# Smaller weight chunks, a fifth staging buffer and two moved waits in the heads of a two-block attention kernel

## The reference, cut to what matters

```python
for _ in range(NB):                                   # NB = 2
    logits = _rms(x, norm_pre_w) @ compete_w.T + compete_b
    vals, idx = top_k(swapaxes(logits, 1, 2), 4)
    wgt = softmax(vals)
    wx = x @ write_w.T + write_b
    ws = _rms(ws + einsum('bsk,bskd->bsd', wgt, gathered(wx, idx)), norm_post_w)
    q = x @ wq.T + bq;  kk = ws @ wk.T + bk;  vv = ws @ wv.T + bv
    att = softmax(einsum('blhd,bshd->bhls', q, kk) * scale)
    x = _rms(x + (att @ vv) @ out_proj_w.T + out_proj_b, norm_post_w)
out = x_in + x
```

## Time and profile before

| | us |
|---|---|
| median of 3 runs | 1086.61 (1082.34 to 1092.57) |
| the profiled execution | 1089.83 |
| its span, first to last instruction | 1087.8 |
| mean granted TensorE clock, share of full | 0.983 |
| first head, block start to first softmax add of its tail | 382.3 to 466.6 |
| second head, the same | 763.9 to 850.9 |
| write projection starts, first and second head | 398.9, 777.9 |
| tile 0's scores on PE (L1032, 16 records), each tail | 3.69 |
| K projection starts, first and second head | 408.2, 787.3 |

### The profile page before, as it was taken

The page is one execution under the profiler, slowest core; times in us unless marked ns, Lnnn a source line. Parts: engine busy times, 40 slices in busy tenths (PEclk is TensorE's granted clock), DMA queues, the critical chain, the costliest instruction groups (busy, mean ns, idle before and its releaser), DMA issues. The chain is left out here.

```text
span 1087.8 us, 14736 instructions
## 1 busy us (share of the span) xinstructions
PE 1017.6 (94%) x4984; PEld 574.4 (53%) x4984; DVE 724.1 (67%) x1004; ACT 574.7 (53%) x960; POOL 458.6 (42%) x214
## 2 busy tenths in 40 slices
PE   2999999999999888999999999997988999999995
PEld 0444444444444334466666666664344666666663
DVE  5999999999999532245555555553423366666664
ACT  3788988888888601235555555555111223333323
POOL 7899999999999310001111111111100033333333
PEclk9999999999999999999999999998898999999998
DMA  4456565656564769835566575646586566868664
GB/s 144 150 178 209 172 215 168 220 163 219 165 217 149 270 233 374 286 130 181 178 231 207 191 246 181 232 155 246 201 338 244 189 216 238 286 229 294 220 228 154
DMA packets 124412, 232.54 MB, mean 214 GB/s; under 512 B 8096, under 2 KB 82976, under 8 KB 122048
## 3 DMA queue, kind: packets, MB, share of 16 engines
q1 hardware_dynamic: 122560, 221.27, 59.1%
q10 hardware_dynamic: 1152, 8.39, 2.2%
q0 software_dynamic: 640, 2.10, 0.7%
HBM read 139.45 MB, written 92.28 MB: 213 GB/s over the span
## 5 line engine op out<-in xcount | busy, mean ns | idle before, releaser
L1032 PE MATMUL bank<-work 128*128 128x256 f32 (+1 forms) x1024 | 244.4, 382 | 3.4 <-DMA work<-x0T_scratch 1.8
L1061 PE MATMUL bank<-work 128*128 128x512 f32 (+1 forms) x512 | 230.3, 592 | 2.1 <-ACT work L1163 1.3
L1032 PEld LDWEIGHTS bank<-work 128*128 128x128 f32 x1024 | 187.2, 190 | 40.5 <-issue 20.6
L1223 POOL TENSOR_TENSOR work<-work 128x1024 f32<-128x1024 f32 x32 | 75.5, 2360 | 236.5 <-DVE work L1145 236.5
L1213 POOL COPY xres<-work 128x1024 f32<-128x1024 f32 x32 | 33.4, 1043 | 328.1 <-DVE work L1145 328.1
L455 PE MATMUL bank<-work,ident 128*128 128x512 f32 x256 | 126.9, 619 | 23.8 <-DVE work L370 22.5
L1061 PEld LDWEIGHTS bank<-work 128*128 128x128 f32 x512 | 97.1, 190 | 97.6 <-issue 91.8
L1096 DVE TENSOR_TENSOR work<-bank,sbias 128x256 f32<-128x256 f32 x64 | 27.2, 424 | 168.4 <-PE bank L1032 168.4
L440 POOL TENSOR_TENSOR work<-work 128x1024 f32<-128x1024 f32 x32 | 85.2, 2662 | 23.7 <-ACT work L355 8.2
L455 PE MATMUL bank<-work 128*128 128x511 f32 x192 | 91.4, 599 | 0.0
L434 POOL TENSOR_SCALAR work<-work 128x1024 f32<-128x1024 f32 x32 | 89.1, 2784 | 3.8 <-DMA work<-in_kT 1.2
(11 more groups left out here) (158 smaller groups left out, 1566.8 us busy)
## 6 DMA issues: line engine op xcount, KB each, us to landing
work<-in_kT SPq DMA_DIRECT2D x32, 512.0 KB, 3.4
work<-in_xT SPq DMA_DIRECT2D x32, 512.0 KB, 3.9
x0T_scratch<-work SPq DMA_DIRECT2D x32, 512.0 KB, 3.2
x_natural_scratch<-xres SPq DMA_DIRECT2D x32, 512.0 KB, 5.1
work<-x0T_scratch SPq DMA_DIRECT2D x32, 512.0 KB, 4.4
x_natural_scratch<-work SPq DMA_DIRECT2D x32, 512.0 KB, 3.1
x1T_scratch<-work SPq DMA_DIRECT2D x32, 512.0 KB, 2.8
work<-x1T_scratch SPq DMA_DIRECT2D x32, 512.0 KB, 4.9
```

Of the source, the lines that this page charges most:

```text
L1032: last = nc.tensor.matmul(ps_s[p], xTb[p][:, c, :], Amat[:, i, :, c * 32:c * 32 + 32], start=(c == 0), stop=(c == NC - 1))
L1061: last = nc.tensor.matmul(ps_o[:, cols], attT[:, k * P:(k + 1) * P], Bmat[k][:, i, cols], start=(k == 0), stop=(k == 1), skip_group_check= ...
L1223: nc.gpsimd.tensor_tensor(x1s[p], x1s[p], xo[p], ALU.add).then_inc(fin, 1)
```

## The change

1. `stream`: the five 2 MB loads become 20 of 512 KB, each with a semaphore per slot and chunk. Chunk a waits until PE has used chunk a of the half before it in that slot (`project` now counts per chunk) and until chunk a of the previous half in the stream has landed, so at most four are under way. PE waits per chunk. The `wo_T` loads become eight of 512 KB.
2. `stageA` gets a fifth buffer (at work[16384]); the copy of pair i waits for the store of pair i - 5.
3. PE waits for the copies of all products before group 2, not before group 0.
4. The stage of group (1, 2) moves to `lgT`, which is also the bias of the first four copies, so that this copy waits for them (`grp_d` 4). Tile 1's buffer is thereby free in the head.
5. SP loads tiles 0 and 1 in the head; PE computes tile 0's scores there in place of three `keep_warm` matmuls; the tail begins without them. SP's `wait_Bm` moves to tile 2.
6. The waits for the stores of x0T and x1T leave the ends of the first stage and of `tail(0)`; they stand now in the head, before SP's `load_x`, and in the second head before POOL's gathers also.

```diff
-        w_in = [stage_sem(head_sems, f"head_weights_in_{i}") for i in range(3)]
-        first_in = [stage_sem(head_sems, f"head_first_weights_in_{i}") for i in range(3)]
+        w_in = [[stage_sem(head_sems, f"head_weights_in_{i}_{a}") for a in range(4)] for i in range(3)]
...
-                sp.wait_ge(x0_out, 16 * NT)
...
-        stageA = [cut(14336 + 512 * i, 512) for i in range(4)]
-        stageB = {(0, 2): cut(8192, 1024), (0, 3): cut(8192, 1024), (1, 2): cut(2048, 1024), (1, 3): cut(8192, 1024)}
+        stageA = [cut(14336 + 512 * i, 512) for i in range(5)]
+        NA = len(stageA)
+        stageB = {(0, 2): cut(8192, 1024), (0, 3): cut(8192, 1024), (1, 2): lgT[:], (1, 3): cut(8192, 1024)}
...
+            stream = ((0, wk_T, 1, wr_ps, 0, 2), (1, wv_T, 0, wr_ps, 1, 2), (2, wv_T, 1, kk_ps, 0, 2),
+                      (0, wq, 0, kk_ps, 1, 3), (1, wq, 1, vv_ps, 0, 3))
...
-                    for slot, w, i, free, count in ((0, wk_T, 1, wr_ps, 1),
-                                                    (1, wv_T, 0, wr_ps, 2), (2, wv_T, 1, kk_ps, 1),
-                                                    (0, wq, 0, kk_ps, 2), (1, wq, 1, vv_ps, 1)):
-                        sp.wait_ge(free, count)
-                        piece(slot, w, i)
+                    for n, (slot, w, i, free, used, load) in enumerate(stream):
+                        for a in range(4):
+                            sp.wait_ge(free, 4 * used + a + 1)
+                            if n > 0:
+                                sp.wait_ge(w_in[stream[n - 1][0]][a], 16 * stream[n - 1][5])
+                            sp.dma_start(ring[slot][:, a, :], w[:, 4 * i + a, :]).then_inc(w_in[slot][a], 16)
...
                             sp.wait_ge(grp_ps, 4)
-                            load_x(sp, t, 0, 0, 0, 0)
+                            sp.wait_ge(x0_out if t == 0 else x1T_out, 16 * NT)
+                            for m in range(2):
+                                load_x(sp, t, 0, m, m, m)
...
                         for c in range(4 * i, 4 * i + 4):
+                            pe.wait_ge(w_in[slot][c % 4], 16 * load)
...
-                        last.then_inc(done, 1)
+                            last.then_inc(done, 1)
...
-                        if hp % 4 == 0:
-                            pe.wait_ge(w_in[hp // 4], 16 * 2)
+                        pe.wait_ge(w_in[hp // 4][hp % 4], 16 * 3)
...
-                    wait_product(pe, HP - 1)
...
+                        if g == 2:
+                            wait_product(pe, HP - 1)
...
                     wait_product(pe, HP - 2)
-                    keep_warm(banks[0], 3)
+                    wait_product(pe, HP - 1)
+                    pe.wait_ge(bias_in[t], 16)
+                    pe.wait_ge(xT_in[t][0], 16)
+                    for c in range(NC):
+                        last = nc.tensor.matmul(banks[0][:, 0:HS], xTb[0][:, c, :], Amat[:, 0, :, c * 32:c * 32 + 32],
+                                                start=(c == 0), stop=(c == NC - 1))
+                    last.then_inc(sc_ps, 1)
...
-                    wait(eng, st_a[i % 4], 16 * (i // 4))
+                    wait(eng, st_a[i % NA], 16 * (i // NA))
...
-                                eng.wait_ge(st_a[j], 16 * 2)
+                                eng.wait_ge(st_a[j], 16 * ((HP - 1 - j) // NA + 1))
...
+                    if (k, b) == (1, 2):
+                        eng.wait_ge(grp_d, 4)
...
+                    if t == 1:
+                        pool.wait_ge(x1T_out, 16 * NT)
...
-                        act.wait_ge(prod_ps, i + 2)
-                        act.dma_start(ring[i // 4][:, i % 4:i % 4 + 2, :], wo_T[:, i:i + 2, :])\
-                            .then_inc(wo_in[i // 2], 16)
+                        for j in (i, i + 1):
+                            act.wait_ge(prod_ps, j + 1)
+                            act.dma_start(ring[j // 4][:, j % 4, :], wo_T[:, j, :]).then_inc(wo_in[j], 16)
...
-                        if not (isinstance(m, int) and m == 0):
+                        if not (isinstance(m, int) and m < 2):
                             wait(sp, sc_ps, m - 1)
                             load_x(sp, t, b, tc, m, p)
+                        if isinstance(m, int) and m == 2:
+                            wait_Bm(sp)
...
-                    wait_Bm(sp)
...
-                        sp.wait_ge(x1T_out, 16 * NT)
...
-                    scores(0, 0, 0)
-                    scores(0, 0, 1)
```

More of the change, by code:

```diff
@@ L552, in head @@
             c_in, np_in, st_s = hsem("constants_in"), hsem("npost_in"), hsem("bias_out")
-            wo_in = [hsem(f"wo_in_{i}") for i in range(4)]
-            st_a = [hsem(f"A_out_{i}") for i in range(4)]
+            wo_in = [hsem(f"wo_in_{i}") for i in range(HP)]
+            st_a = [hsem(f"A_out_{i}") for i in range(NA)]
+            sc_ps = stage_sem(tail_sems, "tail_scores_ps")
             lgt_ps, lgT_ok, dtop, sel_ok, idx_ok = (hsem(x) for x in ("lgt_ps", "lgT", "top", "sel", "index"))
@@ L637, in _ @@
                             sp.wait_ge(grp_ps, 4)
-                            load_x(sp, t, 0, 0, 0, 0)
-                    for i in range(4):
-                        sp.wait_ge(st_a[i], 16 * 2)
+                            sp.wait_ge(x0_out if t == 0 else x1T_out, 16 * NT)
+                            for m in range(2):
+                                load_x(sp, t, 0, m, m, m)
+                    for i in range(NA):
+                        sp.wait_ge(st_a[i], 16 * ((HP - 1 - i) // NA + 1))
                 @block.tensor
@@ L659, in _, with project @@
                     pe.wait_ge(xbt_ok, 2)
-                    def project(ps, xT, i, slot, done):
+                    def project(ps, xT, i, slot, load, done):
                         for c in range(4 * i, 4 * i + 4):
+                            pe.wait_ge(w_in[slot][c % 4], 16 * load)
                             for q in range(Q):
@@ L692, in _ @@
                     pe.wait_ge(wsT_ok, 1)
-                    for i, slot, done, count in ((0, 2, first_in, 4), (1, 0, w_in, 1)):
-                        pe.wait_ge(done[slot], 16 * count)
-                        project(psK, wsT, i, slot, kk_ps)
+                    for i, slot, load in ((0, 2, 1), (1, 0, 2)):
+                        project(psK, wsT, i, slot, load, kk_ps)
                     for i, slot in ((0, 1), (1, 2)):
-                        pe.wait_ge(w_in[slot], 16)
-                        project(psC, wsT, i, slot, vv_ps)
+                        project(psC, wsT, i, slot, 2, vv_ps)
                         if i == 0:
@@ L722, in _ @@
                     pe.wait_ge(sb_ok, 1)
-                    wait_product(pe, HP - 1)
                     for g, (k, b) in enumerate(groups):
                         if g % 4 == 0:
-                            for i in range(2):
-                                pe.wait_ge(wo_in[2 * k + i], 16)
+                            for j in range(4):
+                                pe.wait_ge(wo_in[4 * k + j], 16)
+                        if g == 2:
+                            wait_product(pe, HP - 1)
                         wait_group(pe, g - 3)
@@ L745, in copy_product @@
                         .then_inc(done, 1)
-                    wait(eng, st_a[i % 4], 16 * (i // 4))
-                    copy(stageA[i % 4].rearrange("p (b c r) -> p b c r", b=2, c=NC), new[:, 2:B, :, :])\
+                    wait(eng, st_a[i % NA], 16 * (i // NA))
+                    copy(stageA[i % NA].rearrange("p (b c r) -> p b c r", b=2, c=NC), new[:, 2:B, :, :])\
                         .then_inc(done, 1)
@@ L907, in tail @@
             if first:
-                x1T_out, xt_ps, xt_ev, ssq2_ok, ln2_ok, rs2_ok, l_ps, lp_ok, l2_ps, l_ok = (
-                    tsem(v) for v in ("x1T_out", "x1T_ps", "x1T", "ssq2", "ln2", "rstd2", "l_ps", "lp",
+                xt_ps, xt_ev, ssq2_ok, ln2_ok, rs2_ok, l_ps, lp_ok, l2_ps, l_ok = (
+                    tsem(v) for v in ("x1T_ps", "x1T", "ssq2", "ln2", "rstd2", "l_ps", "lp",
                                       "l2_ps", "logits"))
```

18 lines of the change are left out of this document (8 added, 10 removed).

## The result

Over eleven runs each the changed kernel takes 1076.42 us (1072.92 to 1079.49) and the kernel before 1085.98 (1082.34 to 1092.57): ratio 0.991, 95% interval 0.989 to 0.9931, some 9.6 us or 0.9% faster. A second comparison later gave 0.9935 (0.9912 to 0.9958). The forecast was 1073, from a sum of 14.8 us. The time lies in its range, but just on the "within 1%" side of the line at 1075.7, which had been given a chance of 0.36 against 0.6 for "faster".

What follows compares the result with a forecast made beforehand. PE was taken as the bound, busy 94% of the span, with time to win only in the heads and block ends. Terms summed to 14.8 us: 1075.0 from the profiled execution, 1071.8 from the median; forecast 1073, range 1063 to 1083.

Steps and rivals of the forecast that it cites:

- the line at 1075.7: Whole kernel: below this time the change would count as 1% faster (10.9 us), given a chance of 0.6.
- the three stalls: PE's waits for V's weights: 1.38 and 1.00 us in the first head, 3.53 in the second; all to go.
- A round of 5.6 us: Weight stream in the heads: four 512 KB chunks under way together were taken to land within 5.6 us.
- rival B: Weight stream: four chunks in flight do not keep up, a round takes 8.6 us; about 1098 us, chance 0.05.
- behind them stands only the score bias: SP's queue in the heads: 15 more issues of about 0.35 us delay only the score bias, wanted after the last chunk.
- The head starts at 379.3: 3.0 us gained: First stage's end: without the wait for the last x0T store, PE starts the head at 379.3 instead of 382.32.
- the gathers come only after the top-k: First head: gathers still wait for the row stores but come after the top-k, so no loss was counted.
- Fifth buffer, gate in the groups: Heads: PE's wait moves from before the groups to their middle, some 3 us, until group 1's copy gets its buffer.
- The terms 0.3 + 0.5 and 3.0: Products to tail: gains to DVE's first add, 0.3 us (first head) and 3.0 (second); 0.5 for tile 1's earlier load.
- a bound in the forecast at 1.8 us: Tile 0's scores in the head: if PE falls to half clock before them, the gain is 1.8 us less.
- 2.66 us or more was followed by half clock, 1.38 and 1.00 not: PE in the heads: idle gaps of 2.66 us or more bring half clock, gaps of 1.38 and 1.00 us do not.
- C: Rival: only the plain waits pay, the heads' product-to-tail parts give nothing; 8 us gained, 1079 to 1082 us, chance 0.28.

Runs made afterwards that it cites:

- whole_2mb: The changed kernel with the five weight loads of 2 MB again and no landing wait: 1077.66 us, ratio 0.9942 to the kernel before.
- wk_after_gather: The changed kernel with the first head's first four wk chunks (2 MB) issued behind the gathers: 1081.51 us, ratio 0.9960 to the kernel before.
- four_buffers: The changed kernel with four staging buffers for the A stores instead of five: 1079.59 us, ratio 0.9946 to the kernel before.
- end_waits_back: The changed kernel with the store waits at the ends of the first stage and first tail put back: 1081.27 us, ratio 0.9967 to the kernel before.

## Why the prediction was right, and where its sizes were off

*Weight chunks.* "All have slack, so the three stalls go", products at T + 25.5: measured T + 25.3 in both heads of every kernel with the chunks in this order. The forecast was 2.4 and 5.2 us, the measurement 2.3 and 5.2. A round of 5.6 us was taken; the 20 chunks landed a median of 5.4 us after their issue in either head (3.7 to 6.2 and 4.4 to 7.6), and rival B (8.6) did not come. The 12.8 us for four chunks in a row, an estimate from the Trainium skill's page "DMA: Bandwidth & Descriptors" (anatomy of one DMA), did not come either. The chunks overlap, as these landings show, and the page's formula is a fit of single DMAs on the GpSimd path, while these go out from SP. But "behind them stands only the score bias" and the slack were said with too much ease: what stands behind the chunks is the A stores. `whole_2mb` shows that P to O pays for it, `wk_after_gather` that the stream has no room for 2 MB more.

*End of the first stage.* "The head starts at 379.3: 3.0 us gained" was right: PE starts 0.75 us after F instead of 3.82 (2.93 in the second profile of before). F to M fell by 3.4 to 4.6 us, as the clock held too (L651 takes 1.93 us, L647 took 3.47). The step that failed is the next sentence, that the gathers come only after the top-k and so nothing follows. They come, but into queues that hold 2 MB of wk and the last stores. The first gather is issued at 383.55 and its row is mixed at 388.68:

```profile
383.55 1.17 POOL L786 DMA_INDIRECT work<-x_natural_scratch,gidx  x1 [11.60 <-DVE gidx L826]
```

That is 5.1 us, where it was 3.7, and `wk_after_gather` shows the cause. The first eight warming matmuls don't cover it, and the four behind the gap (eight records) run at half clock in some executions. M to T takes 14.3 to 14.6 us in six profiles without the fall and 16.0 to 16.5 in four with it, against 13.1 before. Net 1.9 us of 3.0.

*Fifth buffer, gate in the groups.* Foretold: group 1's copy at P + 23.9, PE idle some 3 us in the groups. Measured: P + 22.45 and 23.4, with 2.36 and 2.07 us of idle time. The statement that the fifth buffer mostly moves the wait was wrong in its base: it took the waits for the first stores as they were before. They now land late, and `four_buffers` shows what they cost with one buffer less.

*Tile 0 in the head.* The forecast was x issued at P + 28.6 and the first add at P + 39.4; measured were P + 26.9, and 38.3 and 39.5 (41.0 and 39.8 in the second profile). The path is the one named. The terms 0.3 + 0.5 and 3.0 came out as 0.0 and 1.8, for two reasons. The stretches of before, from one execution, were high (second profile: 1.0 and 1.9 less). And the half-clock spell at the scores, a bound in the forecast at 1.8 us, fell in one of the four heads profiled and took 2.95 (6.64 instead of 3.69). The split was wrong too. To the first add, which the terms 0.3 and 3.0 were about, the means of two profiles give a loss of 1.2 and a gain of 0.6 us; tile 1's load, counted at 0.5 and for the first tail alone, gives 1.2 in each (the two are not independent: a later first add leaves less of the wait for tile 1).

*The clock.* "2.66 us or more was followed by half clock, 1.38 and 1.00 not" gave a line that isn't there (see the last section). Of the rivals C was nearest: the plain waits pay, the stretch behind the products little. The measured 1076.42 lies between the forecast's 1073 and C's 1079 to 1082. The sum was 5.2 us too large against the medians: 1.1 us too much at the entry, 2.0 too much behind the products, 0.6 too little at the first tail's end; and some 2.6 us between these two pairs of profiles and the medians. That 1073 is off by only 3.4 is in part luck: it was set between two baselines, 1071.8 and 1075.0.

## What to carry to other kernels

When a stage is fed by DMA all the way, shortening its compute waits moves the start of the next part ahead of its data: follow the landings of the stores and loads behind it before counting the gain, and expect the next gate to take its share. A load that opens the next stage should be issued on the event that frees its buffer, not behind a copy and a small load on the same queue: moving those lines was worth 8.4 +-4.3 us, about as much as the whole change. Take the stage times of a kernel that scatters from two profiles, not one.

## What the hardware showed that I had not expected

TensorE's granted clock falls to 0.50 (1.2 of 2.4 GHz) after some gaps of 2 to 3 us and not after others of the same length. In the groups 2.36 us of idle time were followed by 8.65 us for 64 records, and 2.07 us by 8.77; 2.40, 2.41 and 2.52 us in three other profiles were followed by 7.07. A gap of 2.94 us before the scores left them at 3.69 us (`four_buffers`), one of 2.71 gave 5.38 (`end_waits_back`). Each fall cost 1.4 to 3 us, so a gap of this size on PE's path costs its own length and, in part of the executions, about as much again.

The first gather of rows, issued by POOL on its own queue, was used 5.1 us after its issue where 2 MB of SP's loads had been issued 5.2 us ahead of it. It took 3.7 us where they came behind it (`wk_after_gather`), and also where they had been issued 6.7 us ahead (the kernel before).
